# A four-layer image kernel on one core: biases on a constant feature, centred weights, and work moved between ScalarE, VectorE and GpSimd

## The chip, the core and the metric

The kernel runs on one core of a Trainium2 chip. The metric is the device time in microseconds. A core has a matrix engine (TensorE, PE in the profile; PEld is its weight load), VectorE (DVE), ScalarE (ACT), GpSimd (POOL) and SyncE (SP), which issues DMAs. Each engine runs its own list of instructions in order and waits on semaphores for the others. Matmul results land in PSUM, which here is eight banks: `shared0` to `shared3` and the four of `o_bank`.

## What is computed

The input `x` is 16 images of 64 x 64 pixels with 64 features. Four residual layers follow one another.

```python
x = x + conv0(_ln_c(x))       # 16 images attend to each other at each pixel: 8 heads of 16
t = t + ffn0(_ln_t(t))        # router of 8 experts, the best 2 are mixed
x = x + conv1(_ln_c(x))       # expand to 128, running mean along a column, sigmoid gate, contract
t = t + ffn1(_ln_t(t))        # 32 experts, each picks the 8 best pixels of an image

zn = (z - mu) * rsqrt(var + EPS) * ln_w + ln_b            # conv0
g = sigmoid(zn @ Wg + bg)
att = softmax(einsum(q, k) / 4, axis=1)                   # over the 16 images
out = (einsum(att, v) * g) @ Wo + bo

router_probs = softmax(x @ router_w + router_b)           # ffn0
top_p, top_i = top_k(router_probs, 2); top_p /= sum(top_p)
expert_out = einsum('bnd,edc->bnec', x, expert_w) + expert_b

expanded = einsum(x, W_exp) + b_exp                       # conv1
state_primary, state_gating = split(expanded, 2)
out = einsum(state_primary * sigmoid(ema_scan(state_gating)), W_con) + b_con
# ema_scan: s = s * 0.9 + xi * 0.1 along the column

logits = einsum(x, gate_w) + gate_b                       # ffn1, softmax over the pixels
```

`_ln_c` and `_ln_t` take the mean over the 64 features away and divide by the standard deviation.

## The kernel before

The first three layers and the logits of the fourth need only a column of pixels of all images. So the first stage walks over 64 columns, and each column is cut in two halves of 32 pixels x 16 images = 512 tokens (four tiles of 128). A half column enters per *slot*; there are 128 of them. `STAGES` gives each step a lag in slots: in slot s, the step with lag n works on half column s - n. All engines run one slot after another, and in a slot each runs its steps in the order in which they are written (`TURNS` for TensorE). The first seven pairs of slots are written out, then a hardware loop runs pairs, then the drain of the pipeline (11 slots). Lag, order on each engine, and `BANK` (the PSUM bank of each product) are tables that are written out by hand in the file; nothing is scheduled when it is compiled.

The steps and their names, in the order in which one half column meets them:

- attention: `xload` (DMA), `st_att`, `ag_att` (VectorE: mean and variance), `r1_att`, `sub_att`, `pow_att`, `mul_att` (GpSimd: centre, and scale by variance to the power -1/2), `rnd_att` (ScalarE: round to fp32r), `lo_att` (GpSimd: the rest), `att_t` (transposes), `zT` (ScalarE copy), products `q`, `k`, `v`, `gate`; ScalarE copies `qA`, `km0`, `km1` (keys masked by head, four copies in two pairs), `vA`, `gateA` and `gp1`; `scores`, `smax`, `sub`, `exp`, `ssum`, `rec`, `own`, `probs`, `probsT`, `values`, `og`, `att_out`, and `x1` adds it to `x_bo`, which is x + bo (`xbo`, GpSimd);
- first experts: the same norm (`..._ffn`), `ffn_t`, `tT`, `route`, `lg` (VectorE: logits + router bias), `max`, `top2`, `lgm`, `lge`, `mrep`, `sel`, `gden`, `grec`, `gates`; `y0` to `y3` (all experts of a tile), `yg0` to `yg3` (times gates), `mixed` (the sum over experts, VectorE), `x2`;
- scan: the norm (`..._conv`), `conv_t`, `cT`, `expand`, `exA` (four ScalarE copies), `scan` (VectorE, once per column, in every second slot), `ema` (ScalarE tanh), `gated` (VectorE), `scan_out`, `x3`, which adds it to `x2_bc` = x2 + b_con (`x2bc`, GpSimd);
- logits of the fourth layer: the norm (`..._pick`), `pick_t`, `lT`, `pick`, `picks`; x3 and its normalised form are stored.

An activation matrix is split in a rounded part and a rest, stacked on 128 rows: 64 rows of the rounded part and 64 of the rest. A weight is held as a high and a low part too, so two fp32r matmuls make a product. A bias comes from a matmul of three rows (the bias in three bf16 parts, times ones, `bias3`, `bv3`), from the bias operand of a ScalarE instruction, or from an addition.

TensorE may refill a bank when it has been drained: `bank_free` waits for the last reader of the bank's previous turn. The second stage (from about 2530 us on) selects the pixels, runs the 32 experts and adds; of it the change touches only `pooled_transposed`.

## Time and profile before

| | |
|---|---|
| median of 3 runs | 2711.42 us (2711.4 to 2712.73) |
| profiled execution | 2704.94 us, span 2703.1 us |
| TensorE busy, weight load | 2383.0 us (88%), 1715.2 (63%) |
| VectorE busy | 2245.5 us (83%) |
| GpSimd busy | 2107.5 us (78%) |
| ScalarE busy | 1657.3 us (61%) |
| mean granted TensorE clock | 0.937 of full |
| first and last `mixed` | 89.9 and 2488.4 us |
| moved by DMA | 107.28 MB, mean 40 GB/s |

The busy times are of one profiled execution. The span runs from the first to the last instruction; the execution's own time is 1.8 us longer, and the median of the timed runs 6.5 us above that. Busy shares are means over the loop, its fill and the second stage. A row with "idle before ... <-" tells how long an engine stood before that group and what released it.

### The profile page before, as it was taken

To read this page: it belongs to the slowest core of one execution; us is meant where nothing else is said; L and a number is where in the kernel's file an instruction comes from. 1 tells how busy PE (TensorE), PEld (TensorE's weight loads), DVE (VectorE), ACT (ScalarE), POOL (GpSimd) and SP (SyncE) were. 2 spreads that over 40 slices of the span, in tenths; PEclk is the share of its full clock that TensorE was granted. 3 is DMA by queue.
4 is the path that set the end of the run, shared out by engine and by line. 5 is a ranking of instruction groups with operands and counts; after the bars stand their busy time and mean duration, and the time that the engine had idled before them with its cause. 6 is when DMAs were issued, how large, how long until landed. Compare 5 with 4: busy or idle time off the path is not lost. (4 is left out here: it accounts for less than half of the span.)

```text
span 2703.1 us, 127455 instructions
## 1 busy us (share of the span) xinstructions
PE 2383.0 (88%) x45291; PEld 1715.2 (63%) x45291; DVE 2245.5 (83%) x8757; ACT 1657.3 (61%) x3077; POOL 2107.5 (78%) x3098
## 2 busy tenths in 40 slices
PE   4999999999999999999999999999999999997368
PEld 3666666666666666666666666666666666664258
DVE  3688898898888988889888898888988889886626
ACT  3556666666666666666666666666676666663330
POOL 3677788888888888888888888888888888885310
PEclk9888899999999999999999999999999999996579
DMA  1001111111111111111111111111111111111579
GB/s 22 9 18 22 21 22 20 22 20 21 22 19 23 20 21 22 20 23 20 21 22 20 22 20 21 21 20 23 19 21 22 20 23 20 21 21 16 175 280 373
DMA packets 263185, 107.28 MB, mean 40 GB/s; under 512 B 251284, under 2 KB 253882, under 8 KB 259003
## 3 DMA queue, kind: packets, MB, share of 16 engines
q1 hardware_dynamic: 260831, 101.54, 16.0%
q10 hardware_dynamic: 2268, 4.57, 0.5%
q8 instruction: 57, 0.93, 0.1%
q14 instruction: 29, 0.24, 0.0%
HBM read 55.56 MB, written 50.33 MB: 39 GB/s over the span
## 5 line engine op out<-in xcount | busy, mean ns | idle before, releaser
L516 ACT ACTIVATE kT<-shared,b_k,quarter 128x512 f32<-128x512 f32 x512 | 364.3, 789 | 0.0
L835 DVE TENSOR_TENSOR yg<-shared,gates 128x512 f32<-128x512 f32 x512 | 344.7, 685 | 22.9 <-PE shared L646 22.5
L932 DVE TENSOR_REDUCE mixed<-yg 128x256 f32<-128x2048 f32 x128 | 285.5, 2231 | 0.3
L460 POOL TENSOR_TENSOR probs<-weights,own_den 128x1024 f32<-128x1024 f32 x128 | 247.3, 1932 | 17.0
L645 PE MATMUL shared<-w_expert_hi,tT 128*128 128x512 f32 x512 | 260.5, 509 | 0.0
L653 PE MATMUL shared<-w_o,ogT 128*128 128x64 f32 x2048 | 255.2, 279 | 4.6 <-DVE ogT L975 4.4
L653 PEld LDWEIGHTS shared<-w_o,ogT 128*128 128x128 f32 x2048 | 245.3, 196 | 15.5 <-DVE ogT L975 9.5
L701 PE MATMUL shared<-ident,split_conv 128*128 128x128 f32 x512 | 100.0, 328 | 146.6 <-POOL split_conv L427 146.6
L546 ACT COPY lT<-shared 64x512 f32<-64x512 f32 x128 | 74.1, 579 | 222.5 <-PE shared L674 222.5
L646 PE MATMUL shared<-w_expert_lo,tT 128*128 128x512 f32 x512 | 204.5, 399 | 0.0
L731 PEld LDWEIGHTS o_bank<-probsT,v_sb 32*32 32x32 f32 x16384 | 165.4, 104 | 59.9 <-issue 54.8
L644 PE MATMUL shared<-bias,ones 3*128 3x512 bf16 x512 | 201.6, 394 | 1.0 <-DVE yg L835 0.9
L665 PE MATMUL o_bank<-kT,qT 64*32 64x64 f32 x16384 | 192.8, 228 | 7.0 <-issue 6.4
L731 PE MATMUL o_bank<-probsT,v_sb 32*32 32x64 f32 x16384 | 192.1, 228 | 3.0 <-issue 2.9
L701 PEld LDWEIGHTS shared<-ident,split_conv 128*128 128x128 f32 x512 | 66.5, 164 | 197.0 <-POOL split_conv L427 111.6
L600 ACT ACTIVATE gpre<-shared,bgate_col 64x256 f32<-64x256 f32 x256 | 180.3, 704 | 11.2 <-PE shared L722 5.0
L665 PEld LDWEIGHTS o_bank<-kT,qT 64*32 64x32 f32 x16384 | 171.6, 106 | 16.7 <-issue 8.4
L645 PEld LDWEIGHTS shared<-w_expert_hi,tT 128*128 128x128 f32 x512 | 97.5, 190 | 120.4 <-issue 120.4
L451 POOL TENSOR_TENSOR x<-mixed,x 128x256 f32<-128x256 f32 x128 | 93.0, 727 | 99.0 <-DVE mixed L932 93.0
L956 DVE TENSOR_TENSOR_SCAN ema<-decay,gpre 128x512 f32<-128x512 f32 x64 | 108.3, 1692 | 71.8 <-ACT prim L600 71.8
L551 ACT ACTIVATE gT<-shared,bg_col 128x512 f32<-128x512 f32 x128 | 88.2, 689 | 129.1 <-PE shared L688 129.1
L644 PEld LDWEIGHTS shared<-bias,ones 3*128 3x128 bf16 x512 | 46.7, 91 | 189.8 <-issue 141.9
(200 smaller groups left out, 7139.0 us busy)
## 6 DMA issues: line engine op xcount, KB each, us to landing
x_in<-in_x SPq DMA_DIRECT2D x1024, 16.0 KB, 1.7
x_scratch<-x SPq DMA_DIRECT2D x1024, 16.0 KB, 1.5
normalized_x_scratch<-norm_pick SPq DMA_DIRECT2D x1024, 16.0 KB, 1.4
xa<-normalized_x_scratch SPq DMA_DIRECT2D x8, 1024.0 KB, 8.1
xc<-normalized_x_scratch SPq DMA_DIRECT2D x8, 1024.0 KB, 12.5
out_x<-xc SPq DMA_DIRECT2D x16, 512.0 KB, 5.3
...
xb<-x_scratch SPq DMA_DIRECT2D x4, 1024.0 KB, 17.0
```

Of the source, the lines that this page charges most:

```text
L460: g.tensor_tensor(probs[:], weights[:].unsqueeze(2).broadcast_to([P, 32, 2, 16]), own_den[:].unsqueeze(3).broadcast_to([P, 32, 2, 16]), AL ...
L516: ins = s.activation(kT[:, h, :], bk("k"), ACT.Identity, bias=b_k[:, h:h + 1], scale=quarter[:, h:h + 1])
L600: ins = s.activation(dst, src, ACT.Identity, bias=bias[r0:r0 + D], scale=scale)
L644: t_.matmul(bk(y), ones3[:], bias3[:], start=True, stop=False)
L645: t_.matmul(bk(y), tT[z][:, tile(t)], w_expert_hi[:], start=False, stop=False)
L646: t_.matmul(bk(y), tT[z][:, tile(t)], w_expert_lo[:], start=False, stop=True).then_inc(filled[y], 1)
L653: ins = t_.matmul(bk("att_out")[:, t * D:(t + 1) * D], ogT[:, h, tile(t)], w_o2[:, h, :], start=(h == 0), stop=(h == 1))
L665: ins = t_.matmul(o_bank[g * 32:(g + 1) * 32, u, t * D:(t + 1) * D], qT[z][rows, c, tok:tok + 32], kT[rows, :, tok + c * N:tok + (c + 1) * N],
L701: ins = t_.transpose(bk("conv_t")[:, tile(t)], split["conv"][par(q, "conv_t")][:, t].rearrange("p k d -> p (k d)").bitcast(F32), ident[:])
L731: ins = t_.matmul(o_bank[k * 32:(k + 1) * 32, g, t * 64:(t + 1) * 64], v_sb[z][g * 32:(g + 1) * 32, t, k * 32:(k + 1) * 32], pT[g * 32:(g ...
L835: v.tensor_tensor(yg[:, t], bk(y).rearrange("p (d e) -> p d e", e=NE), gates[:, t, :].unsqueeze(1).broadcast_to([P, D, NE]), ALU.mult).the ...
L932: v.tensor_reduce(mixed[:], yg[:], AX.X, ALU.add).then_inc(s_mixed, 1)
```

## The change

- A normalised token keeps 63 features; feature 64 is the constant 1 in the rounded part and 0 in the rest, set once. This is for attention and first experts. The 64 features of such a token sum to zero, so the last one's weight row is subtracted from the others (`to_rows`), and the freed row holds the bias. The bias of q, k, v, gate, the experts and the router is then in the product.
- The weights of `expand` and `pick` are centred over the features, so conv and pick only scale, with no subtraction.
- `bo` and `b_con` come from a three-row bf16 matmul of 256 columns at the head of `att_out` and `scan_out`. `x_bo` and `x2_bc` become plain copies on ScalarE (`xkeep`, `x2keep`).
- `route` uses a high and a low fp32r weight. `lg` is a ScalarE copy; `lgm` and `gates` go to GpSimd.
- `gated` goes to GpSimd: ScalarE writes tanh + 1 for each half of the rows (`ema1`, with zeros elsewhere) and GpSimd multiplies.
- In the second stage the pooled features are centred, two more ScalarE steps per group.
- Lags, orders and banks are new on every engine.

```diff
 STAGES = {
...
-    2: "xbo own probs km1 vA exp scores smax sub ssum rec",
+    2: "lo_att zT xkeep qA km0 km1 vA att_t q k v scores gate smax sub",
...
-BANK = {"att_out": (2,), "scores": (4, 5), "pick_t": (3,), "scan_out": (1,), "gate": (3,), "y0": (2,), "y3": (3,),
+BANK = {"att_t": (0,), "conv_t": (2,), "pick_t": (3,), "q": (1,), "expand": (2,), "scan_out": (0,), "y2": (1,),
+         "y0": (3,), "k": (0,), "y1": (2,), "values": (4, 5, 6, 7), "y3": (2,), "v": (3,), "ffn_t": (0,), "pick": (1,),
+         "scores": (4, 5), "route": (2,), "gate": (0,), "att_out": (1,)}
...
-                        g.tensor_tensor(norm["conv"][z][:], x2[z][:], mv["conv"][z][:, :, 0:1].broadcast_to([P, QT, D]),
-                                        ALU.subtract).then_inc(s_centered["conv"], 1)
...
-                        g.tensor_tensor(x_bo[z][:], x_in[z][:], bo_rows[:].unsqueeze(1).broadcast_to([P, QT, D]), ALU.add).then_inc(s_xbo, 1)
...
+                    if runs(i, q, "gated"):
+                        z = par(q, "gated")
+                        pool.wait_ge(s_emat, column(i, q, "gated") + 1)
+                        wait(pool, filled["scan_out"], at(i, q, "gated", 2))
+                        half = slice(z * 32, (z + 1) * 32)
+                        g.tensor_tensor(gated[z][:].rearrange("p a (h n) -> p a h n", h=2), ema_own[:, half],
+                                        prim[:, half, :].unsqueeze(2).broadcast_to([P, A // 2, 2, 8]), ALU.mult).then_inc(s_gated, 1)
...
+                        g.tensor_tensor(norm["conv"][z][:], x2[z][:], rstd["conv"][z][:, 1, :].unsqueeze(2).broadcast_to([P, QT, D]),
+                                        ALU.mult).then_inc(s_norm["conv"], 1)
...
-                            ins = s.activation(kT[:, h, :], bk("k"), ACT.Identity, bias=b_k[:, h:h + 1],
-                                               scale=quarter[:, h:h + 1])
+                            ins = s.mul(kT[:, h, :], bk("k"), quarter[:, h:h + 1])
...
+                        s.copy(x_keep[z][:], x_in[z][:]).then_inc(s_xkeep, 1)
...
+                    if par(q, "ema1") == 1 and runs(i, q, "ema1"):
+                        act.wait_ge(s_tanh, column(i, q, "ema1") + 1)
+                        wait(act, s_gated, at(i, q, "ema1", 2))
+                        for h in range(2):
+                            ins = s.activation(ema_own[:, :, h, :], ema_t[:], ACT.Identity, bias=half_of[:, h:h + 1], scale=half_of[:, h:h + 1])
+                        ins.then_inc(s_emat, 1)
...
-                        t_.matmul(bk(y), ones3[:], bias3[:], start=True, stop=False)
-                        t_.matmul(bk(y), tT[z][:, tile(t)], w_expert_hi[:], start=False, stop=False)
+                        t_.matmul(bk(y), tT[z][:, tile(t)], w_expert_hi[:], start=True, stop=False)
...
+                        t_.matmul(bk("scan_out")[:, 0:QT * D], ones3[:], b3[:, 1, :], start=True, stop=False)
...
+                            t_.matmul(bk("route")[:, cols_], tT[z][:, tile(t)], w_router_hi[:], start=True, stop=False)
+                            ins = t_.matmul(bk("route")[:, cols_], tT[z][:, tile(t)], w_router_lo[:], start=False, stop=True)
...
-                            ins = v.scalar_tensor_tensor(gated[z][rows, :, h * 8:(h + 1) * 8],
-                                                         ema_t[rows, half, :], 1.0, prim[rows, half, :], ALU.add, ALU.mult)
...
-                    s.mul(pooled[:, gr, :], banks[2][:, gr * D:(gr + 1) * D], prec[:, gr:gr + 1]).then_inc(s_pool_cp, 1)
+                    s.activation(pooled[:, gr, :], banks[2][:, gr * D:(gr + 1) * D], ACT.Copy, scale=prec[:, gr:gr + 1],
+                                 accum_out=pooled_sum[:, gr:gr + 1]).then_inc(s_pooled, 1)
+                    act.wait_ge(s_pooled, 2 * gr + 1)
+                    s.mul(pooled_sum[:, gr:gr + 1], pooled_sum[:, gr:gr + 1], -1.0 / D).then_inc(s_pooled, 1)
+                    act.wait_ge(s_pooled, 2 * gr + 2)
+                    s.activation(pooled[:, gr, :], pooled[:, gr, :], ACT.Identity, bias=pooled_sum[:, gr:gr + 1]).then_inc(s_pool_cp, 1)
```

How the order moves, at three places. First TensorE, before: the end of one slot's expert products, then the three groups of transposes side by side (`split_conv`, `split_ffn`, `split_att`), each with what it waits for.

```order
L645 MATMUL shared<-w_expert_hi,tT 128x512
L646 MATMUL shared<-w_expert_lo,tT 128x512
L701 MATMUL shared<-ident,split_conv 128x128 [waits split_conv,drained_y3]
L701 MATMUL shared<-ident,split_conv 128x128 x3
L708 MATMUL shared<-ident,split_ffn 128x128 [waits split_ffn,drained_scan_out]
L708 MATMUL shared<-ident,split_ffn 128x128 x3
L715 MATMUL shared<-ident,split_att 128x128 [waits split_att,drained_y2]
```

TensorE after the change, from the transposes of the first experts to the end of a slot.

```order
L752 MATMUL shared<-ident,split_ffn 128x128 [waits split_ffn,drained_k]
L752 MATMUL shared<-ident,split_ffn 128x128 x3
L759 MATMUL shared<-lT,w_pick 32x128 [waits drained_y2,drained_pick_t,pool_setup]
L759 MATMUL shared<-lT,w_pick 32x128 x3
L770 MATMUL o_bank<-kT,qT 32x64 [waits drained_q,drained_k,drained_values,half_keys,pool_setup]
L770 MATMUL o_bank<-kT,qT 32x64 x63
L781 MATMUL shared<-w_router_hi,tT 128x8 [waits drained_ffn_t,drained_y3]
...
L788 MATMUL shared<-zT,w_qkg_hi 128x512 [waits drained_att_t,drained_ffn_t]
L789 MATMUL shared<-zT,w_qkg_lo 128x512
L793 MATMUL shared<-b,ones 128x256 [waits drained_values,drained_pick]
L796 MATMUL shared<-w_o,ogT 128x64 x8
```

`ffn_t` has left the other transposes and stands after the experts and v, and it now waits for the key bank (`drained_k`). Second, ScalarE before: from the last of the four `exA` copies, with `qT` and the four key copies one behind the other.

```order
L600 ACTIVATE prim<-shared,bprim_col 64x256
L608 ACTIVATE qT<-shared,b_qkg 128x16x16 [waits scores_filled,filled_q]
L608 ACTIVATE qT<-shared,b_qkg 128x16x16
L516 ACTIVATE kT<-shared,b_k,quarter 128x512 [waits scores_filled,filled_k]
L516 ACTIVATE kT<-shared,b_k,quarter 128x512
L516 ACTIVATE kT<-shared,b_k,quarter 128x512 [waits scores_filled,filled_k]
L516 ACTIVATE kT<-shared,b_k,quarter 128x512
L533 ACTIVATE picks<-shared,gb_col 128x32x4 [waits filled_pick]
```

ScalarE after, from the same copy, in a slot in which a scan runs.

```order
L576 ACTIVATE prim<-shared,bprim_col 64x256
L520 ACTIVATE kT<-shared,quarter 128x512 [waits scores_filled,filled_k]
L520 ACTIVATE kT<-shared,quarter 128x512
L585 ACTIVATE ema_t<-ema 128x512 [waits ema_tanh,ema_done]
L590 CAST split_ffn<-norm_ffn 128x4x63 [waits filled_ffn_t,normalized_ffn]
L520 ACTIVATE kT<-shared,quarter 128x512 [waits scores_filled,filled_k]
L520 ACTIVATE kT<-shared,quarter 128x512
L599 COPY x_keep<-x 128x256 [waits drained_scan_out,x2_done]
L604 CAST split_conv<-norm_conv 128x4x64 [waits filled_conv_t,normalized_conv]
L609 COPY v_sb<-shared 128x512 [waits o_filled,filled_v]
L615 CAST tT<-shared 128x512 [waits filled_y1,filled_y2,filled_y0,filled_y3,filled_route,filled_ffn_t]
```

`ema_t` (which waits for the scan on VectorE) and the rounding for the first experts now stand between the two pairs of key copies. Third, GpSimd before, around the attention weights.

```order
L451 TENSOR_TENSOR x<-mixed,x 128x256 [waits centered_conv,experts_mixed]
L454 TENSOR_TENSOR own_den<-ssum,odd_even 128x64 [waits denominators]
L460 TENSOR_TENSOR probs<-weights,own_den 128x1024 [waits probs_transposed,own_denominators,exp_done]
L465 TENSOR_SCALAR rstd_conv<-mv_conv 128x4 [waits aggregated_conv,pool_setup]
L470 TENSOR_SCALAR rstd_pick<-mv_pick 128x4 [waits aggregated_pick,pool_setup]
L476 TENSOR_TENSOR x_bc<-x,bcon_rows 128x256 [waits drained_scan_out,x2_done]
```

GpSimd after, at the head of a slot.

```order
L363 TENSOR_TENSOR split_att<-norm_att,split_att 128x4x63 [waits rounded_att,normalized_att]
L370 TENSOR_TENSOR x<-mixed,x 128x256 [waits x2_kept,normalized_conv,experts_mixed]
L376 TENSOR_TENSOR gated<-ema_own,prim 128x512 [waits filled_scan_out,ema_tanh]
L380 TENSOR_TENSOR own_den<-ssum,odd_even 128x64 [waits denominators]
L386 TENSOR_TENSOR probs<-weights,own_den 128x1024 [waits probs_transposed,own_denominators,exp_done]
L391 TENSOR_SCALAR rstd_ffn<-mv_ffn 128x4 [waits aggregated_ffn,pool_setup]
L397 TENSOR_TENSOR gates<-sel,gden 128x32 [waits drained_y2,drained_y1,drained_y3,drained_y0,gate_reciprocal]
```

`gated` and `gates` are new there, before and behind `probs`, and `gates` waits for VectorE's reciprocal.

## Rows read from the trace of the kernel before

**Rows 1.** The reduction `mixed`: duration min/median/max, first and last start.

```profile
L932 DVE TENSOR_REDUCE mixed<-yg x107: 2225/2230/2233, 309.7 to 2297.3; 128x256 f32<-128x2048 f32 x107
...
L932 DVE TENSOR_REDUCE mixed<-yg x128: 2222/2229/2286, 89.9 to 2488.4; 128x256 f32<-128x2048 f32 x128
```

**Rows 2.** Stretches: length, busy (instructions) PE PEld DVE ACT POOL, granted clock, DMA.

```profile
700.00:1100.00 400.00, 366.69 (x7306) 261.03 (x7305) 356.32 (x1435) 269.41 (x502) 345.86 (x513) 0.97 0.12 21
100.00:150.00 50.00, 46.11 (x675) 31.68 (x673) 38.73 (x129) 27.27 (x52) 32.74 (x49) 0.76 0.06 13
1002.36:1039.38 37.02, 33.88 (x684) 23.78 (x683) 33.35 (x136) 25.23 (x47) 32.47 (x49) 1.00 0.13 21
```

**Rows 3.** Waits, 1000 to 1500 us: waiter, waited for, total, times, longest.

```profile
PE shared L701 <- POOL split_conv L427: 33.0, 27, 1.6
...
DVE lg L959 <- PE shared L740: 27.4, 13, 2.6
DVE ema L956 <- ACT prim L600: 15.0, 14, 1.1
...
POOL rstd_conv L465 <- DVE mv_conv L965: 37.7, 27, 1.7
```

**Rows 4.** TensorE in order of time: start, us, line, operands.

```profile
1005.86 1.06 PE L740 MATMUL shared<-w_router,tT 128*128 128x8 f32 x8
...
1008.94 0.38 PE L764 MATMUL shared<-bv,ones 3*128 3x512 bf16 x1 [0.42 <-DVE lg L959]
1009.25 1.16 PE L766 MATMUL shared<-w_scaled,zT 128*128 128x128 f32 x8
1010.39 2.00 PE L653 MATMUL shared<-w_o,ogT 128*128 128x64 f32 x16
1012.32 1.48 PE L665 MATMUL o_bank<-kT,qT 64*32 64x64 f32 x128
1013.73 0.63 PE L674 MATMUL shared<-ident,norm_pick 128*64 128x128 f32 x4
...
1015.77 0.38 PE L644 MATMUL shared<-bias,ones 3*128 3x512 bf16 x1
1016.08 0.50 PE L645 MATMUL shared<-w_expert_hi,tT 128*128 128x512 f32 x1
...
1016.75 0.39 PE L644 MATMUL shared<-bias,ones 3*128 3x512 bf16 x1
```

**Rows 5.** Groups that the change removes: busy, mean ns, idle before.

```profile
L851 DVE SCALAR_TENSOR_TENSOR gated<-ema_t,prim 64x256 f32<-64x256 f32 x256 | 143.2, 559 | 4.0 <-ACT ema_t L523 2.3
...
L358 POOL TENSOR_TENSOR norm_pick<-x,mv_pick 128x256 f32<-128x256 f32 x128 | 107.8, 842 | 4.7 <-DMA normalized_x_scratch<-norm_pick 4.6
...
L385 POOL TENSOR_TENSOR x_bo<-x_in,bo_rows 128x256 f32<-128x256 f32 x128 | 93.5, 730 | 10.6 <-DVE x L860 10.3
...
L959 DVE TENSOR_TENSOR lg<-shared,rb_rows 128x32 f32<-128x32 f32 x128 | 22.5, 176 | 136.7 <-PE shared L740 136.7
```

**Rows 6.** Spread of two of them: duration min/median/max in ns.

```profile
L358 POOL TENSOR_TENSOR norm_pick<-x,mv_pick x128: 609/868/887, 155.6 to 2521.3; 128x256 f32<-128x256 f32 x128
...
L956 DVE TENSOR_TENSOR_SCAN ema<-decay,gpre x64: 1225/1664/2826, 126.9 to 2504.9; 128x512 f32<-128x512 f32 x64
```

**Rows 7.** Groups near in form to what is added or changed.

```profile
L516 ACT ACTIVATE kT<-shared,b_k,quarter 128x512 f32<-128x512 f32 x512 | 364.3, 789 | 0.0
...
L460 POOL TENSOR_TENSOR probs<-weights,own_den 128x1024 f32<-128x1024 f32 x128 | 247.3, 1932 | 17.0
...
L564 ACT CAST split_att<-norm_att 128x256 fp32r<-128x256 f32 x128 | 51.8, 405 | 164.5 <-POOL norm_att L415 164.5
```

**Rows 8.** ScalarE groups between the expansion and the keys.

```profile
L600 ACT ACTIVATE gpre<-shared,bgate_col 64x256 f32<-64x256 f32 x256 | 180.3, 704 | 11.2 <-PE shared L722 5.0
...
L600 ACT ACTIVATE prim<-shared,bprim_col 64x256 f32<-64x256 f32 x256 | 119.9, 469 | 3.2
...
L523 ACT ACTIVATE ema_t<-ema 128x512 f32<-128x512 f32 x64 | 71.6, 1119 | 6.4 <-DVE ema L956 6.4
```

947 lines of the change are left out of this document (476 added, 471 removed).

## The prediction

> **What bounds the kernel now.** I read the busy shares first (the table above): TensorE is busy 88% of the span, VectorE 83%, GpSimd 78%, ScalarE 61%. No engine is full, so the shares alone name no bound. Next I read the pace. All engines walk through "slots" (one half column of pixels enters per slot), and the reduction `mixed` runs once per slot: 107 starts between 309.7 and 2297.3 us are 106 intervals of 18.75 us [rows 1]. The whole run has 128 of them from 89.9 to 2488.4, which is 18.89 each [rows 1]; 127 x 18.75 = 2381 of the 2703 us of the span is this loop, and that is where the change is made. The rest is about 90 us before the first `mixed` and 215 us of drain and second stage after the last.
>
> Then the busy time of two slots without a clock dip [rows 2]: in 37.02 us (18.51 a slot) TensorE is busy 33.88, VectorE 33.35, GpSimd 32.47, ScalarE 25.23. So per slot 16.94, 16.68, 16.24 and 12.6. The slot is 18.51 though TensorE needs 16.94, so 1.57 is idle. The waits say where [rows 3]: in 500 us (27 slots) TensorE stands 33.0 us, 1.2 a slot, before the transposes of the third normalisation, for GpSimd's `split_conv`; GpSimd stands 37.7 us for VectorE's `mv_conv`; VectorE stands 27.4 us for TensorE's router product and 15.0 for ScalarE's gate input. This is a ring of three almost full engines, and a slot gets shorter only if all of the ring is unloaded. The mean interval of 18.75 is 0.24 above 18.51; the granted clock over 700 to 1100 us is 0.97 where it is 1.00 over those two slots [rows 2], so I put the 0.24 down to short spells at the lower level (1.2 GHz).
>
> **The change, engine by engine, per slot.**
>
> TensorE. Out: the four bias matmuls of the experts (start to start 0.31 each [rows 4]) and the one of v (1008.94 to 1009.25, also 0.31 [rows 4]): -1.55. In: two bias matmuls of 256 columns for `att_out` and `scan_out`. Half of a 512-column one is 0.16; they can't cost less than nothing nor more than the wide one, so 0 to 0.62, taken 0.32. The router's four fp32 products (8 passes, 1.06 [rows 4]) become eight rounded ones, each with its own weight load. The number of passes stays, so I take 0 and keep -0.5 to +0.5. Sum -1.2: TensorE needs 15.7.
>
> VectorE. Out: `gated`, two of 0.559 [rows 5]; `lg` (0.176 [rows 5]), and `lgm` and `gates` of the same 32 elements, taken like it. That is 1.12 + 0.53 = -1.65, so 15.0 left. Nothing is added.
>
> GpSimd. Out: `x_bo` and `x_bc`, 0.73 each (the row of `x_bo` [rows 5]), and the two subtractions for conv and pick. The pick one is 0.842 in the mean, its minimum 0.609 [rows 5, 6]; the conv one is of the same form, taken at that minimum. Together -2.9. In: `gated` as one product of 512 elements. Rows bound it by 0.730 (`x_bo`, 256 elements [rows 5]) and 1.932 (`probs`, 1024 [rows 7]); on the line between, 1.13, and 1.2 taken. `gates` and `lgm` of 32 elements are between 0.18 (rounded up from the 0.176 that VectorE takes for one [rows 5]) and the 0.730, taken 0.25 each. Sum -2.9 + 1.7 = -1.2: about 15.0 left.
>
> ScalarE. In: two copies of 128x256 (0.405 as the cast [rows 7]), two selecting passes over `ema_t` per two slots, at most the 0.789 of the key copies [rows 7], so 0.79 a slot, and the copy of the router's result (0.2). +1.8. Out: the bias operand of four key and two query copies. The key copy is 0.789 with two column operands; without one it can save between 0 and 0.2 each, taken 0.1: -0.6. ScalarE goes to 13.8 and stays the least loaded.
>
> Weight set-up has fewer loads and more dependent steps: -2 us, between -5 and +5. The second stage gets two small ScalarE steps per group, on its path only after the last group: +1 us (0 to 3).
>
> **What is late next.** After the load is off, the slot is at least 15.7 (TensorE). I laid the new order out by hand with the durations of the rows, starting where `att_out` of the slot before ends (0). The order shown in the section on the change puts `ema_t` between the key copies km0 and km1 on ScalarE, and TensorE's `ffn_t` reuses the bank that km1 empties. In a slot with a scan: att_t, conv_t, zT, cT, lT, xkeep and qA bring ScalarE to 3.8; exA is 2 x (0.704 + 0.469) = 2.35 [rows 8], 6.2; the scan 1.66 [rows 6], 7.9; `ema_t` 1.12 [rows 8], 9.1; rnd_ffn 0.4 and km1 1.4 (two of 0.79, overlapping), 10.8. Then TensorE has ffn_t 0.6, pick 0.6, scores 1.41 (1012.32 to 1013.73), route 1.0, gate 0.67 (as the pair of an expert, 1016.08 to 1016.75) and `att_out` 1.93 + 0.16 [rows 4], all back to back: 17.2. In a slot without a scan the gate on `ffn_t` is GpSimd's `lo_ffn`. It follows scan_out, x3, grec, gates, and then nine GpSimd steps, at about 10.1, which gives 16.4. The mean is 16.8. Nothing in this layout makes the scan slower than its median, but here it runs beside busy GpSimd, where it has taken up to 2.83 [rows 6]; half of that surplus, in every second slot, is 0.3. So 17.1, which holds the 0.24 of the clock only in part; I let the two uncertainties cancel. The saving is 18.75 - 17.1 = 1.65 a slot.
>
> **The sum.** 118 slots x 1.65 = -195. Ten slots of fill and drain, which are bound by one item's latency and not by load, at half or less, with the drain's shorter chains (two GpSimd steps less in conv and pick): -10. Set-up -2, second stage +1. Together -206. The profiled execution took 2704.9 (span 2703.1 and 1.8 around it), so it would be 2499; the median of the runs is 6.5 above it, 2711.4, and gives **2505**. The likeliest case alone runs from 2460 to 2560 (0.4 a slot each way).
>
> The row that speaks for a cost on the port is the pick subtraction: 609 ns at its least, 868 in the median, standing beside VectorE's `gated` [rows 5, 6], and the scan with 1225, 1664 and 2826 ns [rows 6]. The Trainium skill ("SBUF — State Buffer", Who interferes with whom) says that a VectorE instruction with two SBUF inputs contends with a GpSimd instruction that reads SBUF. The rows agree. By it the removal of `gated` from VectorE frees GpSimd's neighbours, while the scan, now beside GpSimd work in every second slot, loses more; the second half is the first rival below.
>
> For the copies the Trainium skill ("ScalarE: Activation LUTs", What ACT_TABLE_LOAD costs) gives about 93 ns for each per-partition operand. By its figure, an estimate, the six copies save 0.56 a slot. No row here shows the same copy with one operand less.
>
> **Rivals.**
> 1. The port. The scan at 2.8 instead of 1.7 is +1.1 in every second slot, straight into km1 and `ffn_t`, and GpSimd's own steps beside it, 0.26 longer as the pick subtraction is, for four or five of them, hold `lo_att` and so the next slot: +1.1. Together half of 2.2 on top of 16.8 is 17.9; less where they overlap, 17.7. Saving 1.05: -124 - 8 = about 2580. For it: the rows named. Against it: the scan before starts while `probs` runs, and is only 1.66. Chance 0.18.
> 2. The new order fits better than my layout. TensorE is bound by its own 15.7, with 0.24 of clock and hardly a gap: 16.0 a slot, -2.75 x 118 = -325, 2385. For it: 15.0 on the two others. Against it: in the layout km1 and `lo_ffn` both leave TensorE waiting. Chance 0.08.
> 3. The change takes load off but the ring doesn't get shorter. One bank ring, att_t, zT, scan_out, x3, k, km1, ffn_t, tT, gate, gateA, passes three engines inside a slot. If handoffs cost 0.15 more each than I allow (ten of them, 1.5), the slot is at 18.6 and nothing is left: 2700, between 2670 and 2740. Against it: the ring of before has handoffs of the same kind and I have used starts from the trace that contain them. Chance 0.08.
> 4. Slower by the clock. The place is TensorE's waits, which the new order spreads over the slot: before y1, y3 and `ffn_t` instead of one before conv_t. Where TensorE was interrupted in more places, in the fill at 100 to 150 us, it was granted 0.76 [rows 2]. If the loop had a mean of 0.84, TensorE's 15.7 would be 18.7, with 1.1 of waiting 19.8: +1.05 a slot, +124, 2835. It decides from a mean clock of 15.7 / (18.75 - 1.1) = 0.89 down. For it: that window. Against it: over 700 to 1100 us, with as much idle time, 0.97. Chance 0.08.
>
> **How the numbers follow.** Main case 0.58, rivals 0.18, 0.08, 0.08, 0.08. The predicted time is the main case's, 2505. From 2410 to 2650 the range holds the main case and rival 1 and the upper part of rival 2, and leaves out rivals 3 and 4 and a little below, about 0.19. A change within 0.2% (5.4 us) can't be told from none. Faster: main, rivals 1 and 2 and 0.03 of rival 3, 0.87. Within 0.2%: 0.02. Slower: 0.03 of rival 3 and rival 4, 0.11.
>
> **What would show it.** The interval of `mixed` at 17.1 (16.7 to 17.5). TensorE busy at 15.7 a slot, its idle time before `ffn_t` (for kT or for `split_ffn`) and not before conv_t; `mixed` intervals alternating, with the longer slot the one with the scan. GpSimd's `gated` near 1.2; its busy time near 15. ScalarE's kT copy at about 0.7. The scan's median tells rival 1 (2.8 or 1.7), the granted clock rival 4 (0.84 or 0.97). I am wrong in the mechanism if the longest waits of TensorE are for something that isn't in these rings, or if an engine other than TensorE, GpSimd and VectorE is busy over 15 a slot.

## The result

| | before | after |
|---|---|---|
| median | 2711.41 us (2711.01 to 2712.73, 4 runs) | 2482.21 us (2472.55 to 2486.27, 4 runs) |
| ratio, 95% interval | 1 | 0.9149 [0.9121, 0.9176] |
| profiled execution, span | 2704.94, 2703.1 | 2472.55, 2470.8 |
| a slot in the steady loop | 18.75 us | 17.07 us (forecast 17.1) |
| TensorE, VectorE, GpSimd, ScalarE busy per slot | 17.2, 16.7, 16.2, 12.6 | 15.6, 15.6, 15.0, 13.3 |
| granted clock, 700 to 1100 us | 0.97 | 0.98 |

The change makes the kernel 8.5% faster. The forecast was 2505 us in a range of 2410 to 2650.

The reduction `mixed` once per slot, after: in a window of the steady loop, and over the whole run (duration min/median/max, first and last start).

```profile
L990 DVE TENSOR_REDUCE mixed<-yg x106: 2261/2268/2276, 299.6 to 2091.5; 128x256 f32<-128x2048 f32 x106
L990 DVE TENSOR_REDUCE mixed<-yg x128: 2261/2269/2287, 76.7 to 2259.9; 128x256 f32<-128x2048 f32 x128
```

105 intervals in 1791.9 us are 17.07 each. Against [rows 1] the 127 intervals of the whole run take 2183.2 us instead of 2398.5, which is 1.70 less each.

The stretch of [rows 2] after, then two slots from one `mixed` to the next, without and with a scan (length, busy PE PEld DVE ACT POOL, granted clock):

```profile
700.00:1100.00 400.00, 364.25 (x7930) 286.43 (x7929) 365.26 (x1468) 312.50 (x644) 351.49 (x540) 0.98 0.14 23
...
999.35:1015.67 16.32, 14.38 (x335) 11.43 (x320) 15.76 (x64) 13.07 (x28) 14.23 (x22) 1.00 0.14 24
1015.67:1033.25 17.58, 16.14 (x358) 12.40 (x362) 15.37 (x65) 13.50 (x29) 15.81 (x26) 1.00 0.13 23
```

The intervals of `mixed` alternate, 16.3 and 17.6, and the longer one holds the scan. Who waits for whom after, 1000 to 1500 us, which is 29 slots (waiter, waited for, total, times, longest):

```profile
ACT split_conv L604 <- POOL norm_conv L445: 33.1, 29, 1.3
ACT zT L540 <- PE shared L679: 26.7, 29, 1.5
PE shared L752 <- POOL split_ffn L439: 26.1, 29, 1.1
...
POOL rstd_ffn L391 <- DVE mv_ffn L925: 19.0, 15, 1.3
...
DVE x L936 <- PE shared L712: 17.4, 21, 1.0
POOL gates L397 <- DVE gden L939: 16.3, 29, 0.8
```

The wait for `split_conv` of [rows 3] has gone. TensorE's longest wait is now 0.9 us a slot for `split_ffn`, the transpose that the forecast named. VectorE's waits of [rows 3] for the router's product and the gate input have gone too; its longest is now x3's wait for TensorE's `scan_out` (L712), 0.6 us a slot. GpSimd stands almost only for VectorE, for `mv_ffn` (1.3 us in every second slot) and `gden` (0.6 a slot).

The spread of three operations after (ns, min/median/max):

```profile
L376 POOL TENSOR_TENSOR gated<-ema_own,prim x128: 1262/1274/1292, 134.1 to 2288.6; 128x512 f32<-128x512 f32 x128
L955 DVE TENSOR_TENSOR_SCAN ema<-decay,gpre x64: 1172/1182/1215, 122.3 to 2277.7; 128x512 f32<-128x512 f32 x64
L908 DVE SCALAR_TENSOR_TENSOR sel<-marked,lge x128: 172/1532/1880, 67.1 to 2251.6; 128x32 f32<-128x32 f32 x128
```

Two groups of ScalarE, 700 to 1100 us (busy, mean ns, idle before):

```profile
L520 ACT ACTIVATE kT<-shared,quarter 128x512 f32<-128x512 f32 x96 | 60.6, 682 | 5.1 <-PE shared L724 4.6
...
L626 ACT ACTIVATE ema_own<-ema_t,half_of 128x512 f32<-128x512 f32 x22 | 16.5, 810 | 0.0
```

`gated` takes 1.27 us (1.2 taken). The scan is shorter than before, 1.18 against the 1.66 of [rows 6]. What grew is `sel`, a VectorE instruction of 32 elements that the forecast doesn't mention: 0.17 at its least and 1.53 in the median, where the kernel before has 0.165 in the median. The timelines of two engines, in a slot without a scan and in the next one, with a scan, show why.

```profile
1006.50 1.93 POOL L386 TENSOR_TENSOR probs<-weights,own_den 128x1024 f32<-128x1024 f32 x1
...
1006.61 1.87 DVE L908 SCALAR_TENSOR_TENSOR sel<-marked,lge 128x32 f32<-128x32 f32 x1
1008.40 0.59 DVE L913 BATCH_NORM_STATS2 bn_ffn<-x 128x6 f32<-128x64 f32 x4
...
1023.66 0.18 DVE L908 SCALAR_TENSOR_TENSOR sel<-marked,lge 128x32 f32<-128x32 f32 x1
1023.66 1.97 POOL L386 TENSOR_TENSOR probs<-weights,own_den 128x1024 f32<-128x1024 f32 x1 [0.22 <-POOL own_den L380]
...
1027.80 1.18 DVE L955 TENSOR_TENSOR_SCAN ema<-decay,gpre 128x512 f32<-128x512 f32 x1
1028.44 0.54 POOL L411 TENSOR_SCALAR rstd_conv<-mv_conv 128x4 f32<-128x4 f32 x1
```

In the first slot `sel` starts 0.11 us after GpSimd's `probs` and ends with it, at 1008.48 against 1008.43. Behind it on VectorE stand the statistics and `gden`, for which GpSimd waits. In the second it starts together with `probs` and takes 0.18. Between 300 and 2100 us both kinds are there 53 times: `sel` takes 1.59 to 1.88 us where it starts 0.09 to 0.39 after `probs`, and 0.17 or 0.18 where the two start within 0.01 of each other. In the second slot it is GpSimd's small `rstd_conv` that is held: it starts while the scan runs and ends with it, 0.54 us instead of 0.19.

### The profile page after: what moved, and what is told of

Its sections match the earlier page's. It is cut to its first block and busy times, and to the rows that moved or that the text cites. A ratio compares the mean times of both kernels' runs of the same rounds, so it can differ in the third digit from the quotient of the medians.

```text
span 2470.8 us, 126806 instructions
## 1 busy us (share of the span) xinstructions
PE 2159.8 (87%) x44905; PEld 1709.2 (69%) x44905; DVE 2109.1 (85%) x8121; ACT 1757.0 (71%) x3597; POOL 1958.5 (79%) x2984
## 5 line engine op out<-in xcount | busy, mean ns | idle before, releaser
L520 ACT ACTIVATE kT<-shared,quarter 128x512 f32<-128x512 f32 x512 | 322.9, 682 | 34.5 <-PE shared L724 32.4
L770 PE MATMUL o_bank<-kT,qT 64*32 64x64 f32 x16384 | 232.4, 228 | 10.1 <-issue 9.1
L735 PE MATMUL o_bank<-probsT,v_sb 32*32 32x64 f32 x16384 | 190.4, 226 | 21.3 <-issue 21.1
L752 PE MATMUL shared<-ident,split_ffn 128*128 128x128 f32 x512 | 80.7, 280 | 109.1 <-POOL split_ffn L439 109.0
L976 DVE TENSOR_TENSOR ogT<-o_bank,gT 128x512 f32<-128x512 f32 x256 | 163.7, 681 | 5.5 <-PE o_bank L735 5.5
L540 ACT CAST zT<-shared 128x512 fp32r<-128x512 f32 x128 | 75.0, 586 | 124.8 <-PE shared L679 124.7
L376 POOL TENSOR_TENSOR gated<-ema_own,prim 128x512 f32<-128x512 f32 x128 | 163.0, 1274 | 0.7 <-ACT ema_own L626 0.7
L949 DVE STREAM_TRANSPOSE probsT<-probs 128x1024 f32<-128x1024 f32 x128 | 155.1, 1212 | 3.5 <-POOL probs L386 3.5
L604 ACT CAST split_conv<-norm_conv 128x256 fp32r<-128x256 f32 x128 | 51.9, 406 | 145.8 <-POOL norm_conv L445 145.8
L746 PEld LDWEIGHTS shared<-w_v,zT 128*128 128x128 f32 x1024 | 131.8, 194 | 24.7 <-DVE yg L870 17.7
L712 PE MATMUL shared<-w_con,gated 128*128 128x64 f32 x1024 | 147.5, 289 | 0.0
## 6 DMA issues: line engine op xcount, KB each, us to landing
xb<-x_scratch SPq DMA_DIRECT2D x4, 1024.0 KB, 17.1
```

The lines of the kernel that those rows point to most:

```text
L376: g.tensor_tensor(gated[z][:].rearrange("p a (h n) -> p a h n", h=2), ema_own[:, half], prim[:, half, :].unsqueeze(2).broadcast_to([P, A / ...
L520: ins = s.mul(kT[:, h, :], bk("k"), quarter[:, h:h + 1])
L735: ins = t_.matmul(o_bank[k * 32:(k + 1) * 32, g, t * 64:(t + 1) * 64], v_sb[z][g * 32:(g + 1) * 32, t, k * 32:(k + 1) * 32], pT[g * 32:(g ...
L770: ins = t_.matmul(o_bank[g * 32:(g + 1) * 32, u, t * D:(t + 1) * D], qT[z][rows, c, tok:tok + 32], kT[rows, :, tok + c * N:tok + (c + 1) * N],
L976: ins = v.tensor_tensor(by_group(ogT[:, h, :]), o, by_group(gT[z][:]), ALU.mult)
```

## Experiments

Ratios are to the kernel before on the same chip. A slot is always the mean interval of `mixed` in the steady loop. "At full clock" means the intervals between two `mixed` whose granted clock is 0.995 or more, counted one by one; any other interval has a spell at half clock (1.2 instead of 2.4 GHz) in it. Neighbouring intervals alternate in length, so a *pair*, two in a row, is the safer measure where the two are not disturbed alike. Between 300 and 2100 us a pair without a spell takes 37.0 us before and 33.9 after; spells are in 36 of 95 intervals before and in 22 of 105 after.

**The kernel again.** No edit.

> The changed kernel as it is, beside the three below on one chip, as the base for small differences. Both theories expect about 2480 us and a ratio to the kernel before of 0.915.

2474.1 us, ratio 0.9148 [0.9098, 0.9198]. The result repeats.

**`sel` behind the statistics.** On VectorE `sel` moves from ahead of `bn_ffn` to behind the aggregates.

```diff
-                    if runs(i, q, "sel"):
...
                     if runs(i, q, "ag_ffn"):
...
+                    if runs(i, q, "sel"):
```

> The changed kernel with one step moved on VectorE: sel, and with it nothing else, from behind st_conv to behind ag_ffn. In every second slot sel took 1.87 us instead of 0.18, and it ended when GpSimd's probs ended. Theory A (port): sel is held by probs for as long as probs runs, wherever the row before it ends. Behind ag_ffn it starts about 1.2 us later and ends at the same moment, so ag_ffn is 1.8 us earlier, GpSimd no longer waits 1.3 us for mv_ffn in those slots, and split_ffn comes earlier until km1 is the last. Expected: sel 0.8 us at most in those slots, a slot 0.2 to 0.4 us shorter on average, 2430 to 2460 us. Theory B (the time of sel is of its own, from its operands or from waiting for lge): sel keeps 1.87 us in those slots and the total stays within 10 us of 2480.

2452.22 us, ratio 0.9043 [0.9004, 0.9082], slot 16.96. The time is in theory A's range; the slot is only 0.11 us shorter, where theory A had 0.2 to 0.4. `sel` is at 0.82 in the median and GpSimd's wait for `mv_ffn` is gone. `sel` still ends with `probs`; it only starts later, now in every slot 1.0 to 1.4 us after `probs`. The wait for `gden` rose from 16.3 to 30.1 us in 500.

**`lge` in PSUM.** ScalarE writes `lge`, one of the two inputs of `sel`, to free columns of a PSUM bank. The order doesn't change.

```diff
-            lgm, lge, sel = cb("lgm", [P, QT, NE]), cb("lge", [P, QT, NE]), cb("sel", [P, QT, NE])
+            lgm, sel = cb("lgm", [P, QT, NE]), cb("sel", [P, QT, NE])
+            lge = o_bank[:, 3, 512 - QT * NE:512].rearrange("p (t e) -> p t e", e=NE)
```

> The changed kernel with one operand of sel in another memory: ScalarE writes lge to 32 free columns of a PSUM bank, so sel reads one operand from SBUF (marked) and one from PSUM. The order is untouched. Theory A (the port that VectorE's second SBUF operand shares with GpSimd is held by probs): sel takes about 0.2 us in every slot, with the minimum and the median alike, VectorE's busy time falls by 0.8 us a slot, and the total comes to 2420 to 2450 us. Theory B (sel is long because of its place or because it waits for lge): the median of sel stays near 1 us or alternates between 0.18 and 1.87 as before, and the total stays at 2475 us.

2446.76 us, ratio 0.9044 [0.8998, 0.9089]. The spread of `sel` with `lge` in PSUM:

```profile
L909 DVE SCALAR_TENSOR_TENSOR sel<-marked,o_bank x128: 164/170/189, 66.0 to 2224.0; 128x32 f32<-128x32 f32 x128
```

Its waits at x3 and at `gates`, 1000 to 1500 us:

```profile
DVE x L937 <- PE shared L713: 35.0, 29, 2.0
...
POOL gates L398 <- DVE gden L940: 30.0, 29, 1.9
```

With one input outside SBUF `sel` is 0.17 to 0.19 each time, though it starts up to 0.4 us after the same `probs`, as it does in the kernel after. That is the port. The Trainium skill ("SBUF — State Buffer", Who interferes with whom) says that a VectorE instruction with two SBUF inputs contends with a GpSimd instruction that reads SBUF; the trace agrees, 1.53 against 0.17 in the median. The loop gains only 0.17 a slot, to 16.90. VectorE's x3 now waits longer for TensorE's `scan_out` (1.2 us a slot, from 0.6), and `grec`, for which `gates` waits, is queued behind x3. The clock takes its part too: a pair without a spell is 33.1 us, 0.4 a slot less than after, but 32 of 105 intervals have a spell, and a pair with one takes 34.3. In a slot with a spell x3 stands 2.12 us for `scan_out` (at 978 us), in one of the same kind without it 1.01 (at 1148 us).

**The same, and x3 behind `grec` and `ag_att`.**

```diff
-                    if runs(i, q, "x3"):
...
                     if runs(i, q, "grec"):
...
                     if runs(i, q, "ag_att"):
...
+                    if runs(i, q, "x3"):
```

> The run with lge in PSUM, and in addition VectorE's x3 is moved behind grec and ag_att in its own order, so that gden and grec, which GpSimd waits for before gates (30.0 us in 29 slots in the run with lge in PSUM), no longer stand behind x3, which waits for TensorE's scan_out (35.0 us in 29 slots). Theory C (the slot is now closed through GpSimd: x3, gden, gates, split_ffn, TensorE): gates starts about 1 us earlier, the 1.0 us a slot of waiting there goes, split_ffn is ready earlier and the slot comes from 16.90 down to 16.2 to 16.5: 2360 to 2410 us. Theory D (x3 is itself in the ring: x3, k, TensorE's next projections): x3 runs later by the two small instructions put ahead of it, the slot stays at 16.8 to 17.1 and the time at 2430 to 2475 us.

2363.39 us (2361.93 to 2372.47), ratio 0.8718 [0.8692, 0.8744]. It beats both kernels, and time and slot are in theory C's range. Its `mixed` in the steady loop:

```profile
L991 DVE TENSOR_REDUCE mixed<-yg x111: 2260/2267/2286, 302.2 to 2088.2; 128x256 f32<-128x2048 f32 x111
```

110 intervals in 1786.0 us are 16.24 each. A stretch of it, and then all waits of GpSimd over 1 us in 500 us (31 slots):

```profile
1100.00:1500.00 400.00, 377.20 (x8264) 294.05 (x8249) 370.00 (x1549) 329.06 (x679) 375.14 (x567) 1.00 0.14 24
```

```profile
POOL probs L387 <- POOL own_den L381: 3.5, 16, 0.2
POOL rstd_pick L430 <- DVE mv_pick L961: 1.5, 1, 1.5
```

GpSimd's waits for `gden` and `mv_ffn`, 1.2 us a slot in the kernel after, are gone. It is busy 15.2 of 16.2 us, and TensorE (15.3) and VectorE (15.0) are as full. Of the 0.66 us a slot between this run and the last, some 0.4 are in the pairs without a spell (32.3 us in the mean instead of 33.1); the rest comes with fewer spells, 9 of 110 intervals instead of 32 of 105. Why there are fewer is not shown.

**Four bias matmuls back.** A zero matmul of 512 columns ahead of each expert product, 1.24 us a slot of TensorE.

```diff
+                        t_.matmul(bk(y), ones3[:], zero3[:], start=True, stop=False)
-                        t_.matmul(bk(y), tT[z][:, tile(t)], w_expert_hi[:], start=True, stop=False)
+                        t_.matmul(bk(y), tT[z][:, tile(t)], w_expert_hi[:], start=False, stop=False)
```

> The changed kernel with a matmul of three rows and 512 columns (of zeros) back in front of each expert product, 1.24 us more of TensorE a slot. Theory L (TensorE's own load sets the slot): the slot grows by all of it, 17.07 to 18.3 us, 2630 us. Theory R (TensorE waits 0.9 us a slot for split_ffn behind these products, so the ring through GpSimd sets the slot and the matmuls come out of that wait): 0.3 to 0.5 us a slot, 17.5 us, 2510 to 2540 us, and the wait for split_ffn almost gone.

2492.4 us, ratio 0.9202 [0.9163, 0.924]. The stretch from 700 to 1100 us:

```profile
700.00:1100.00 400.00, 392.43 (x7909) 291.06 (x7908) 367.63 (x1477) 309.69 (x644) 351.75 (x538) 0.99 0.13 23
```

TensorE is busy 392 of 400 us and the slot is 17.07, the same as without them; a pair without a spell is 33.9 us too. So theory L is out, and even theory R's 0.3 to 0.5 didn't come; TensorE's wait for `split_ffn` fell from 26.1 to 7.8 us in 500, as theory R had it. TensorE's own load doesn't bound the kernel after. The rest, 10 us in the medians and 22 between the two profiled executions, comes outside the steady loop.

**`gated` back on VectorE**, as the two products of before, and `ema1` (ScalarE) out.

```diff
-                        g.tensor_tensor(gated[z][:].rearrange("p a (h n) -> p a h n", h=2), ema_own[:, half],
-                                        prim[:, half, :].unsqueeze(2).broadcast_to([P, A // 2, 2, 8]), ALU.mult).then_inc(s_gated, 1)
...
+                            ins = v.scalar_tensor_tensor(gated[z][rows, :, h * 8:(h + 1) * 8],
+                                                         ema_t[rows, half, :], 1.0, prim[rows, half, :], ALU.add, ALU.mult)
```

> The changed kernel with gated back on VectorE, in front of x1, as two products straight from ema_t, and without the two selecting passes on ScalarE. VectorE gets 1.15 us more a slot, GpSimd 1.27 less, ScalarE 0.8 less. Theory L (a load counts wherever it lies, and VectorE has 15.6 us): VectorE has about 1.2 us of waiting a slot, and gated lies in front of x1, on the path to k and to gates: +0.5 us a slot or more, 2540 us and over, with x2 and split_att of GpSimd stretched by the port. Theory O (GpSimd's load was what held the ring): the slot gets shorter or stays, 2440 to 2480 us.

2542.64 us, ratio 0.9399 [0.936, 0.9438], slot 17.66, as theory L had it. The move is worth 0.59 us a slot, 60 us in the medians, of the gain. VectorE is busy 386 of 400 us, and GpSimd, with 314, now waits for it at two places:

```profile
POOL own_den L374 <- DVE ssum L890: 42.2, 28, 1.5
POOL rstd_ffn L385 <- DVE mv_ffn L923: 35.5, 28, 1.3
```

**The two subtractions back on GpSimd**, straight ahead of `mul_conv` and `mul_pick`.

```diff
+                        g.tensor_tensor(norm["conv"][z][:], x2[z][:], mv["conv"][z][:, :, 0:1].broadcast_to([P, QT, D]),
+                                        ALU.subtract).then_inc(s_cc, 1)
+                        pool.wait_ge(s_cc, at(i, q, "mul_conv"))
```

> The kernel after with two GpSimd subtractions put back directly in front of mul_conv and mul_pick (about 1.2 to 1.45 us a slot on GpSimd; weights stay centred, so that they change nothing but the load). GpSimd goes from 15.0 to about 16.3 us busy of 17.07. Theory G (GpSimd is in the ring that closes the slot now): the slot grows by 0.6 to 1.3 us, 2555 to 2640 us. Theory O (they lie in GpSimd's waits for gden and mv_ffn, 1.2 us a slot together): the slot grows by less than 0.3, up to 2520 us.

2672.94 us (2665.36 to 2683.13), ratio 0.9854 [0.9821, 0.9887]. 1.25 us more on GpSimd, at this place in its order, give 1.73 us a slot, 18.80, and take back some 190 of the 229 us of the change. That is more than the 0.6 to 1.3 of theory G. GpSimd's load is in the ring that closes the slot. Two neighbouring slots:

```profile
1002.11:1020.89 18.78, 17.11 (x335) 14.00 (x320) 15.94 (x64) 13.59 (x28) 15.36 (x25) 0.82 0.13 22
1020.89:1039.64 18.75, 16.41 (x358) 12.48 (x362) 15.36 (x64) 13.14 (x27) 17.17 (x27) 1.00 0.12 20
```

VectorE and GpSimd in order of time, in the first of them:

```profile
1013.60 0.15 DVE L936 TENSOR_REDUCE gden<-sel 128x4 f32<-128x32 f32 x1
1014.73 0.42 DVE L943 TENSOR_TENSOR x<-shared,x_keep 128x256 f32<-128x256 f32 x1 [0.99 <-PE shared L719]
1015.07 0.17 DVE L946 RECIPROCAL gden<-gden 128x4 f32<-128x4 f32 x1
...
1015.32 0.24 POOL L398 TENSOR_TENSOR gates<-sel,gden 128x32 f32<-128x32 f32 x1 [1.30 <-DVE gden L946]
```

Every second slot has a mean clock of 0.82. There TensorE's passes between `split_att` and `scan_out` run at half clock (1008.49 to 1013.24 in its timeline, against 1027.97 to 1031.05 in the next slot, 1.7 us longer). x3 waits for `scan_out`, the reciprocal is queued behind x3, and GpSimd stands 1.30 us at `gates`, where the kernel after stood 0.22 in the slot of 1010 us. Over the pair, GpSimd stands 1.71 us at `gates` (1.30 and 0.41) against 0.88 (0.22 and 0.66) after, so 0.83 of the 0.96 us that a pair costs beyond the subtractions' own time is this wait. That it comes from the half clock is a reading, not a test.

**Both loads back.** The subtractions and the four zero matmuls together (the two edits above).

> The kernel after with both loads added: the two GpSimd subtractions in front of mul_conv and mul_pick (alone they brought the slot from 17.07 to 18.80 us and the steady clock from 0.98 to 0.91) and the four zero bias matmuls in front of the expert products (1.24 us a slot of TensorE, which alone left the slot at 17.07 and brought the steady clock to 1.00). Theory K (1.25 us of the 1.73 us that the subtractions cost is GpSimd's own time, and 0.5 us is that TensorE's passes run at the half clock in part of the slots, because TensorE now stops and waits): the matmuls fill the stops, the steady clock comes to 0.97 or more, and the slot falls to 18.2 to 18.5 us, 2600 to 2650 us, faster than with the subtractions alone although more is done. Theory L (the stops are part of the ring, and the clock is only their sign): the matmuls lengthen TensorE's part, the slot is 18.8 or more and the time 2675 to 2800 us.

2693.6 us, ratio 0.9943 [0.9919, 0.9968]. The slot is 18.79.

```profile
1014.85:1034.76 19.91, 19.67 (x362) 14.96 (x354) 16.07 (x64) 13.55 (x29) 16.39 (x27) 0.83 0.13 21
1034.76:1052.39 17.63, 16.74 (x346) 12.26 (x342) 15.23 (x64) 12.97 (x27) 16.17 (x25) 1.00 0.12 21
```

Theory K fell: the clock stays at 0.83 in every second slot. Theory L has the number but not the mechanism, since a pair of slots is 37.54 us with the matmuls and 37.53 without, so TensorE isn't what sets the pair. Whether the 0.48 us a slot would go if the clock stayed up is not shown by either run.

**The kernel before without its five bias matmuls** (it leaves the biases of v and the experts out).

```diff
-                        t_.matmul(bk(y), ones3[:], bias3[:], start=True, stop=False)
-                        t_.matmul(bk(y), tT[z][:, tile(t)], w_expert_hi[:], start=False, stop=False)
+                        t_.matmul(bk(y), tT[z][:, tile(t)], w_expert_hi[:], start=True, stop=False)
...
-                        t_.matmul(bk("v"), ones3[:], bv3[:], start=True, stop=False)
```

> The kernel before with one thing taken off: the five bias matmuls of the experts and of v, 1.55 us of TensorE a slot. It leaves those biases out. Theory L: TensorE's load makes the slot, 18.75 to 17.2 us, 2515 us. Theory R (the ring through GpSimd makes it): TensorE's wait for split_conv grows from 1.2 to more than 2.3 us a slot, the slot stays at 18.3 or more, 2650 to 2710 us, and if the granted clock falls with the longer waits as it did in the run with the old order and the new load, slower than that.

2727.08 us, ratio 1.0071 [1.0036, 1.0105], slot 19.20. TensorE has 1.55 us less to do and the kernel is slightly slower. Theory R had the slot; the wait for `split_conv` grew to 2.1 us a slot, not to more than 2.3. The clock is 0.89 from 700 to 1100 us and 0.91 over the loop (0.97 before), and 62 of 93 intervals have a spell. The few pairs without one (6) take 36.0 us, 0.5 a slot less than before.

**The kernel before without the two subtractions** (conv's and pick's inputs are not centred).

```diff
-    6: "sub_conv mul_conv lo_conv x2bc rnd_conv cT exA conv_t expand scan",
+    6: "mul_conv lo_conv x2bc rnd_conv cT exA conv_t expand scan",
```

> The kernel before without GpSimd's two subtractions of the mean (norm_conv and norm_pick); everything else stands as it was. It leaves out the centring of the conv's and the pick's input. GpSimd loses two instructions, about 1.45 us a slot by their means of 0.6 to 0.9 us. Theory G (GpSimd's part of the chain norm, split, TensorE held the slot of 18.75 us): the slot falls to 17.7 to 18.2 us and the time to 2590 to 2650 us. Theory O (the order of the engines held it, and the subtractions lay in waits): the slot stays within 0.2 of 18.75, 2685 to 2730 us.

2782.8 us, ratio 1.0254 [1.0206, 1.0302], slot 19.35. Both theories missed: less work, and a longer slot. The intervals show where it is. First three slots of the kernel before, the last with a short spell at half clock, then two of this one:

```profile
1020.91:1039.38 18.47, 17.00 (x343) 12.11 (x344) 16.08 (x68) 12.83 (x25) 16.98 (x26) 1.00 0.13 22
1039.38:1057.93 18.55, 16.88 (x341) 11.68 (x339) 17.28 (x69) 12.39 (x24) 15.51 (x24) 1.00 0.12 20
1057.93:1077.29 19.36, 18.09 (x343) 13.50 (x344) 16.07 (x68) 12.81 (x25) 16.95 (x26) 0.91 0.13 21
```

```profile
1009.88:1027.01 17.13, 16.45 (x339) 11.45 (x337) 16.88 (x68) 11.83 (x24) 13.98 (x22) 1.00 0.11 19
1027.01:1048.12 21.11, 19.75 (x347) 15.01 (x345) 18.10 (x69) 12.95 (x26) 15.56 (x24) 0.84 0.12 21
```

The intervals at full clock fell from 18.47 (59 of 95) to 17.13 (44 of 92). That is not yet a gain of 1.34 us: no pair here is free of a spell, and an interval can be short because its neighbour is long. The run with both loads shows that: 17.6 at full clock beside 19.9, in a pair as long as that of two times 18.8 in the run with the subtractions alone. A pair takes 38.7 us in the mean here, against 37.0 without and 37.9 with a spell before. What theory G would give at full clock is open. What the timeline shows is that in every second slot TensorE stands before a bias matmul and is then granted half the clock:

```profile
1033.57 0.38 PE L753 MATMUL shared<-bv,ones 3*128 3x512 bf16 x1 [1.36 <-DVE lg L948]
1033.88 1.39 PE L755 MATMUL shared<-w_scaled,zT 128*128 128x128 f32 x8
1035.07 3.63 PE L642 MATMUL shared<-w_o,ogT 128*128 128x64 f32 x16
1038.63 2.05 PE L654 MATMUL o_bank<-kT,qT 64*32 64x64 f32 x128
```

`att_out` takes 3.63 us where [rows 4] has 2.00, and the scores 2.05 where they have 1.48. 38 of the 92 intervals have a mean clock between 0.7 and 0.85 and are 21.1 to 22.5 us long, 4 us and more longer than their neighbours. That the half clock is what makes the kernel slower is read from this; no run holds the clock fixed.

**The new work in the old order.** The kernel before with most of the work of its loop removed and moved as in the change, in the tables of before (the removed biases and the centring are left out, and `lg`, `lgm`, `gates` and the router stay as they were).

```diff
-    7: "ema",
+    7: "ema ema1",
...
+                        s.copy(x_bo[z][:], x_in[z][:]).then_inc(s_xbo, 1)
```

> The kernel before, with its own orders, lags and banks, but most of the load of the changed one: no bias matmuls for the experts and v, two of 256 columns at att_out and scan_out, no subtraction for conv and pick, x_bo and x2_bc as ScalarE copies, gated on GpSimd with the two selecting passes on ScalarE. It leaves out the biases of the experts, v, bo and b_con and the centring of conv and pick; lg, lgm, gates and the router stay as they were (0.5 us a slot on VectorE stays). Theory L (the load makes the time): the ring of three engines loses 1.2 to 1.65 us a slot on each, so 17.3 us a slot, about 2530 us, ratio 0.93. Theory O (the order makes it): TensorE's wait for split_conv grows by what its matmuls lose, 18.3 us a slot or more, 2650 us and over, ratio 0.98.

2791.14 us, ratio 1.0284 [1.0229, 1.034], slot 19.62.

```profile
1015.63:1032.89 17.26, 15.24 (x336) 11.24 (x335) 16.03 (x66) 12.13 (x25) 14.11 (x21) 1.00 0.14 23
1032.89:1053.87 20.98, 18.70 (x343) 14.54 (x344) 17.49 (x68) 15.58 (x29) 14.91 (x22) 0.84 0.10 18
```

I had also put the copy for `xbo` behind `v_sb` on ScalarE, where it adds a wait (for x1, 25.5 us in 500), and GpSimd's `gated` waits 26.2 us for the selecting passes. Yet the picture is the same: 17.26 at full clock (31 of 91 intervals), and 20.9 to 23.6 at a mean of 0.7 to 0.85 (38 of 91). Lighter engines alone, placed like this, don't make the kernel faster.

**The old work in the new order.** After, with the loads of before put back by zeros, `x_keep` on GpSimd.

```diff
+                        g.tensor_tensor(x_keep[z][:], x_in[z][:], zero_rows[:].unsqueeze(1).broadcast_to([P, QT, D]), ALU.add).then_inc(s_xkeep, 1)
```

> The changed kernel, with its orders, lags and banks, but the load of the kernel before: matmuls of three rows and 512 columns (of zeros) back in the four expert products and v, none at att_out and scan_out, the two subtractions back, x_keep and x2_keep as additions on GpSimd (behind lo_ffn), gated, lg, lgm and gates on VectorE, no selecting passes. It leaves out bo and b_con. The router stays on eight rounded products. Theory L: back near the time before, 18.3 to 18.9 us a slot, 2650 to 2730 us. Theory O: the gain mostly stays, 17.5 us a slot or less, under 2560 us.

3329.07 us, ratio 1.2286 [1.2237, 1.2336]. Inconclusive. I had put `x_keep` so late on GpSimd that the buffer of the next input comes free late, and VectorE stands for the DMA that fills it, which the new order alone wouldn't do:

```profile
DVE bn_att L982 <- DMA x_in<-in_x: 91.0, 21, 6.1
```

What the new order does with more load is read from the two runs with the subtractions back instead.

## Why the prediction was right

**The bound.** A ring of three engines was right. Which of them counts was not known then. TensorE's load is not in it (four matmuls more: 0 a slot). GpSimd's is (subtractions: +1.73 for 1.25), and so is VectorE's (`gated` back: +0.59; `sel` freed: -0.17). Order counts as much: with x3 behind the reciprocal, which moves no load, it is -0.83. The forecast's "the slot is at least 15.7 (TensorE)" is met (busy 15.6), but it didn't bind.

**The layout by hand** had the right transpose, `ffn_t`, and the wrong instruction in front of it in a slot with a scan. It had `km1` there, the second pair of key copies behind `ema_t`:

```profile
1021.63 0.60 PE L679 MATMUL shared<-ident,split_att 128*128 128x128 f32 x4
...
1030.40 1.26 ACT L520 ACTIVATE kT<-shared,quarter 128x512 f32<-128x512 f32 x2
...
1031.57 0.72 POOL L439 TENSOR_TENSOR split_ffn<-norm_ffn,split_ffn 128x252 fp32r<-128x252 f32 x1
...
1032.44 0.63 PE L752 MATMUL shared<-ident,split_ffn 128*128 128x128 f32 x4 [0.79 <-POOL split_ffn L439]
```

Counted from the transpose behind `att_out` (L679), as the layout counts, `km1` ends at 10.0 us (forecast 10.8) and GpSimd's `split_ffn` at 10.7, and TensorE goes on after the latter. In a slot without a scan `split_ffn` ends at 10.9 (forecast 10.1), behind the long `sel`. From one L679 to the next a slot with a scan takes 16.8 us and one without 17.1 where no spell disturbs them; the layout had 17.2 and 16.4. So the slot without the scan is the longer one for TensorE. The intervals of `mixed` (17.6 with the scan, 16.3 without) look as forecast because they cut the pair at another place.

The 0.3 for the port was for a scan that it makes longer. The scan became shorter: its 1.66 of [rows 6] already held a wait, since in the kernel before it starts at 1007.13 us while `probs` runs to 1007.72. The port took 1.7 us by way of `sel` in about half of the slots instead, and freeing `sel` was worth 0.17 a slot. The spells at half clock add 0.12 (a pair of 33.9 us becomes 34.4 in 22 of 52). That 16.8 plus 0.3 came so near to 17.07 is luck in part: the slot with the scan was taken 0.4 too long and the other 0.7 too short. The forecast asked only which long instruction the port would hit, not which short one has two SBUF inputs beside `probs`.

**Prices.** `gated` 1.27 (1.2), `gates` and `lgm` 0.24 (0.25), TensorE 15.6 a slot (15.7), GpSimd 15.0 (15.0), ScalarE 13.3 (13.8). VectorE has 15.6 instead of 15.0, by `sel` (0.98 in the mean, from 0.18); with `lge` in PSUM it is at 14.8. A selecting pass takes 0.81, a little over the "at most 0.789". The key copy with one operand less went from 789 to 682 ns, 107 less (0.1 taken); the Trainium skill ("ScalarE: Activation LUTs", What ACT_TABLE_LOAD costs) has about 93 for it.

**The sum.** Measured 2472.55 - 2704.94 = -232 between the profiled executions, forecast -206. Three terms were mis-sized:
- Loop: -215 over all 127 intervals. The forecast had -195 for 118 and half the gain or less for ten of fill and drain. They gained as much as the others.
- Ahead of the first `mixed`: -13.2, where -2 was for the set-up. The first `x_in` DMA starts 4.3 us earlier (8.7 against 13.0), and the first transposed `probs` comes 2.0 us after `probs` (38.1 and 36.1) instead of 9.1 (49.2 and 40.1). The new order also shortens the first item's way through the pipe.
- Behind the last `mixed`: -3.8, forecast +1. To the first selection it is 2.7 longer (46.9 against 44.2); the rest of the second stage is 6.5 shorter, at a granted clock of 0.90 against 0.87. Neither is traced to its cause, so the +1 for the second stage is neither confirmed nor refuted.

**The rivals.** The port (1) exists, on another instruction. TensorE's bound (2) is not reached. "The ring doesn't get shorter" (3) didn't happen in the new order. The clock (4) was the live one: in the old order with less load the clock from 700 to 1100 us fell to between 0.89 and 0.91 and the slot grew to between 19.20 and 19.62. That the one made the other is the likeliest reading, by the passes at half clock in those slots; no run separates them. In the new order 22 of 105 intervals have a spell at half clock too, but a pair of slots with one takes 34.4 us instead of 33.9 (16.99 and 17.43, against 16.32 and 17.58):

```profile
1033.25:1050.24 16.99, 15.84 (x336) 13.02 (x321) 15.95 (x63) 13.31 (x28) 14.35 (x22) 0.90 0.13 22
1050.24:1067.67 17.43, 16.00 (x358) 12.27 (x360) 15.37 (x64) 13.54 (x29) 15.66 (x26) 1.00 0.14 24
```

**What the gain is made of.** Less load alone: slower by 2.8% (with my placement of the copies). The new order with the subtractions' load: 1.5% faster. Both: 8.5%. The new order with the whole old load is not measured in a usable way, so the share of the order alone is open. The forecast spoke of load and latency separately and added them, and that worked only because both came together. The same sum made for a part alone, in the old order, would have been wrong in its sign: TensorE's part gave +0.7% and the subtractions' +2.5%.
